# Row scatters to 64 experts: GpSimd waits for every two of them before it sends the next two

## The chip, the core and the metric

The kernel runs on one core of a Trainium2 chip. The metric is the device time of one execution in microseconds (us). Before the change three runs took 3416.25, 3429.02 and 3433.31 us, with a median of 3429.02.

## What is computed

The program is a chain of eleven layers over x, 4096 tokens of 128 numbers. The change touches two of them, the first and the second, which are mixtures of 64 experts with a shared expert. The reference of such a layer, cut to what matters here:

```python
logits = x @ wg.T                            # 4096 tokens, 64 experts
gates = softmax(logits)
w_topk, idx_topk = top_k(gates, 8)           # eight experts for each token
w_topk = w_topk / w_topk.sum(-1)
rank  = position of the token in the list of its expert
valid = rank < 160                           # capacity of an expert
buf   = zeros(64, 160, 128).at[expert, rank].set(x[token])
h     = einsum("ech,efh->ecf", buf, expert_w1); x1, x2 = split(h)
out   = einsum("ecf,ehf->ech", x1 * silu(x2), expert_w2)
combined = zeros(4096, 128).at[token].add(w * out[expert, rank])
y = shared_expert(x) + combined
```

The program computes x = x + 0.5 * moe(layernorm(x)), then a block attention with 8 heads over blocks of 64 tokens, then the same kind of mixture again, and after that eight layers of other kinds.

## The kernel before

The tokens stand in SBUF as 32 tiles of 128 rows. Routing goes over them in 8 groups of 4 tiles. For each group VectorE computes statistics, normalized rows, gates, the eight largest, and for each row eight slot numbers (`idx`, written at L1932). A slot is a place in a table `rows` of 10240 slots (64 experts of 160) in HBM. GpSimd then writes the rows to their slots: `pool_scatter` issues, for each of the 4 tiles and each of the 8 choices, one indirect DMA of 128 rows (L1814), so 32 scatters for a group. Rows whose slot number is out of bounds are dropped. Below, such an indirect DMA is called a scatter.

`pool_send` (L1818) calls it. The first three groups (`SURE` is 3) are always sent, with two semaphores `early` in turn. Each later group is sent only if some expert is not full yet (L1831), with the semaphore `sent`, and GpSimd waits for its 32 scatters at its end (L1833). In the trace five groups are sent in the first mixture (160 scatters) and four in the second (128). The group buffers `row` and `idx` are eight deep, as many as there are groups, so no group waits for a buffer to come free.

The first mixture's routing is a stage of its own (`routing_alone`, names l0f1r). Beside it VectorE runs the steps of a state kernel for a later layer, and SP clears HBM tables. The second mixture's routing runs beside the block attention (`block_attention`, names l0a). There GpSimd's stream also holds the additions of the attention's output bias to x (`pool_residual`, L2101), 16 of them, in program order with the sends: two of them follow the first send, one follows the second. Each stage ends only when all engines are through, GpSimd with its last scatters too. Then the stage of the experts (names l0f1e, l0f2e) loads the rows back from HBM, computes, and adds the results to a table with scatters of its own (L2986, 80 rows each).

In two later layers (names l3f1a, l3f2a) another class does routing to 8 experts, with 8 scatters for a group. The change doesn't touch it.

Of the kernel before, what the change touches and what calls it, by code (L numbers as in the profile page):

```python
# [802 lines left out]
class RoutingApart:  # L803
# [6 lines left out]
    DEPTH, LATE = 4, 4  # L810
    PER = 16 * TPG * K

# [51 lines left out]
    def pool_send(self, g, n):  # L864
# [10 lines left out]
        if n:  # L875
            g.wait_ge(self.sent[1 - n % 2], self.PER * ((n + 1) // 2))
            g.sem_inc(self.rows_free, 1)
# [876 lines left out]
class Routing:  # L1754
# [6 lines left out]
    DEPTH = 8  # L1761
    NONE = 65536.0
    SURE = -(-SLOTS // (K * GT))
    PER = 16 * TPG * K

    def __init__(self, ph, c, m, front, logits, hidden, out, kept=GROUPS):
# [40 lines left out]
        g.sem_inc(self.rows_free, self.DEPTH)  # L1807
        self.last_slot = g.to_reg(SLOTS - 1)

    def pool_scatter(self, g, n, sent):  # L1810
        u = n % self.DEPTH
        for t in range(TPG):
            for j in range(self.K):
                g.indirect_dma_start(out=self.m.rows, out_offset=bass.IndirectOffsetOnAxis(  # L1814
                    ap=self.idx[u][:, t, j:j + 1], axis=0), in_=self.row[u][:, t, :], in_offset=None,
                    bounds_check=self.last_slot, oob_is_err=False).then_inc(sent, 16)

    def pool_send(self, g, n):  # L1818
        g.wait_ge(self.rows_ready, TPG * (n + 1))
        g.wait_ge(self.idx_ready, n + 1)  # L1820
        if n == 0:
            g.wait_ge(self.m.rows_cleared, self.m.ROWS_CLEARED)
        if n < self.SURE:
            self.pool_scatter(g, n, self.early[n % 2])
            if n:
                g.wait_ge(self.early[1 - n % 2], self.PER * ((n + 1) // 2))
                g.sem_inc(self.rows_free, 1)
            return
        g.wait_ge(self.full_ready, n - self.SURE + 1)
        least = g.value_load(self.full[n % self.DEPTH][0:1, 0:1], min_val=0, max_val=TOKENS)  # L1830
        with g.If(least < self.CAP):  # L1831
            self.pool_scatter(g, n, self.sent)
            g.wait_ge(self.sent, self.PER * (n - self.SURE + 1))  # L1833
        if n == self.SURE:
            g.wait_ge(self.early[1 - self.SURE % 2], self.PER * ((self.SURE + 1) // 2))
            g.sem_inc(self.rows_free, 1)
        g.sem_inc(self.rows_free, 1)
# [79 lines left out]
    def dve_slots(self, v, n):  # L1917
# [4 lines left out]
                               op0=ALU.is_lt, op1=ALU.mult)  # L1922
        if n >= self.SURE:
            V.tensor_reduce(self.least[:, :], self.rank[:, 0:E], AX_X, ALU.min).then_inc(self.least_ready, 1)
# [2311 lines left out]
```

## Time and profile before

| | before |
|---|---|
| median of 3 runs | 3429.02 us |
| the profiled execution, first to last instruction (its span) | 3818.2 us |
| TensorE busy in it | 2748.8 us |
| VectorE busy | 2054.0 us |
| ScalarE busy | 1399.8 us |
| GpSimd busy | 1883.3 us |
| mean granted TensorE clock | 0.819 |

The trace is of one execution, and it is the only one whose inside is seen. The page gives its span and no total for what lies around it. The span is 389 us longer than the median of the runs. Busy time counts the running of instructions, not their waits; for a scatter GpSimd is busy while it makes the transfer's descriptors, and not while the data moves. A stretch of the trace is shown with the busy time and the number of instructions of each engine in it, in the order TensorE, its weight loads, VectorE, ScalarE, GpSimd. After these come the granted TensorE clock (1.00 is 2.4 GHz, 0.50 is 1.2 GHz), the busy share of the 16 DMA engines, and GB/s.

### The profile page before, as it was taken

The numbers are of one execution on the slowest core, as the hardware profiler recorded it, in microseconds if no ns is written. First come the engines' busy times: TensorE is split into PE (matmuls) and PEld (weight loads), VectorE is DVE, ScalarE is ACT, GpSimd is POOL, SyncE is SP. The second block draws the span as 40 slices with busy tenths as digits, with TensorE's granted clock in tenths as the row PEclk, the third lists the DMA queues.
The fourth block names the chain that finished last, engine by engine and source line by source line (L and its number), as shares of the span: only waits on it lengthen the run. The fifth ranks groups of instructions, "written<-read, shape, count | busy, mean of one in ns | idle before, by whom it ended". The sixth has DMA issues, their size and how long they took to land. (4 is left out here: it accounts for less than half of the span.)

```text
span 3818.2 us, 69208 instructions
## 1 busy us (share of the span) xinstructions
PE 2748.8 (72%) x24495; PEld 1757.8 (46%) x24514; DVE 2054.0 (54%) x6095; ACT 1399.8 (37%) x2956; POOL 1883.3 (49%) x2224
## 2 busy tenths in 40 slices
PE   1226994543889565889988999764688876998763
PEld 1114883332578533555546554453233333555453
DVE  4356334432623354468854776312699998776313
ACT  1111221210222131436643655323667662654323
POOL 5651774345057531249973123354588885133354
PEclk7667997665799877979978998687799997998586
DMA  9101994110069674111000101122212120110123
GB/s 364 34 1 38 222 223 101 50 57 10 26 168 221 167 248 117 69 19 18 18 6 12 21 21 27 36 70 74 84 56 89 45 89 13 19 27 23 35 73 92
DMA packets 222726, 294.16 MB, mean 77 GB/s; under 512 B 36704, under 2 KB 179583, under 8 KB 216288
## 3 DMA queue, kind: packets, MB, share of 16 engines
q1 hardware_dynamic: 168544, 245.65, 20.6%
q0 software_dynamic: 47616, 39.44, 5.5%
q10 hardware_dynamic: 6272, 5.24, 0.6%
q8 instruction: 173, 2.83, 0.3%
q14 instruction: 121, 0.99, 0.1%
HBM read 181.88 MB, written 107.12 MB: 76 GB/s over the span
## 5 line engine op out<-in xcount | busy, mean ns | idle before, releaser
L3694 POOL TENSOR_TENSOR l3am_db<-l3am_du,l3am_bs 128x512 f32<-128x512 f32 x256 | 318.4, 1274 | 44.9 <-DVE l3am_hh L3915 44.1
L4034 PE MATMUL l3am_y<-l3am_hc,ident 128*128 128x512 f32 x512 | 280.7, 631 | 82.1 <-DVE l3am_hc L3923 81.0
L3915 DVE TENSOR_TENSOR_SCAN l3am_hh<-l3am_dA,l3am_db 128x512 f32<-128x512 f32 x256 | 299.7, 1206 | 21.4 <-ACT l3am_dA L3824 12.0
L1161 POOL TENSOR_TENSOR l2a_pT<-l2a_pT,kept 128x512 int32<-128x512 int32 x224 | 278.7, 1278 | 63.1 <-ACT l2a_pT L1367 63.1
L2986 POOL DMA_INDIRECT l0f_table<-l0f2e_y,l0f2e_idx x128 | 178.9, 1398 | 179.3 <-DVE l0f2e_idx L2958 131.8
L2986 POOL DMA_INDIRECT l0f_table<-l0f1e_y,l0f1e_idx x128 | 178.9, 1398 | 144.2 <-DVE l0f1e_idx L2958 96.4
L1248 DVE CUSTOM_DVE_ANT_0 l2a_junk<-l2a_s,addend 128x256 f32<-128x256 f32 x512 | 188.3, 421 | 65.4 <-PE l2a_s L1484 60.3
L1814 POOL DMA_INDIRECT l0f_rows<-l0f1r_row,l0f1r_idx x160 | 160.0, 1000 | 104.1 <-issue 69.5
L1241 DVE TENSOR_REDUCE l3f2a_mx<-l3f2a_s 128x2 f32<-128x512 f32 x256 | 166.2, 685 | 55.2 <-PE l3f2a_s L1484 53.2
L1367 ACT ACTIVATE l3f2a_pT<-l3f2a_e 128x512 f32<-128x512 f32 x256 | 141.8, 596 | 144.1 <-PE l3f2a_e L1501 113.4
L1367 ACT ACTIVATE l3f1a_pT<-l3f1a_e 128x512 f32<-128x512 f32 x256 | 141.7, 596 | 142.7 <-PE l3f1a_e L1501 100.2
L1241 DVE TENSOR_REDUCE l3f1a_mx<-l3f1a_s 128x2 f32<-128x512 f32 x256 | 165.8, 685 | 52.4 <-PE l3f1a_s L1484 50.3
L4034 PEld LDWEIGHTS l3am_y<-l3am_hc,ident 128*128 128x128 f32 x512 | 94.7, 198 | 206.7 <-DVE l3am_hc L3923 147.6
L3824 ACT ACTIVATE l3am_dA<-l3am_dl,l3am_al 128x512 f32<-128x512 f32 x256 | 167.3, 682 | 58.4 <-POOL l3am_dl L3683 29.8
L1501 PE MATMUL l2a_e<-l2a_qk 32*128 32x256 f32 x1024 | 178.0, 429 | 11.3 <-DVE l2a_pT L1169 11.3
L1501 PE MATMUL l3f2a_e<-l3f2a_qk 32*128 32x256 f32 x1024 | 181.6, 450 | 2.7 <-issue 2.0
L1484 PE MATMUL l3f2a_s<-l3f2a_qk 32*128 32x256 f32 x1024 | 180.3, 452 | 3.4 <-issue 2.4
L1484 PE MATMUL l3f1a_s<-l3f1a_qk 32*128 32x256 f32 x1024 | 177.7, 442 | 6.4 <-issue 3.1
L1501 PE MATMUL l3f1a_e<-l3f1a_qk 32*128 32x256 f32 x1024 | 180.2, 443 | 1.0 <-ACT l3f1a_pT L1367 0.6
L1484 PE MATMUL l2a_s<-l2a_qk 32*128 32x256 f32 x1024 | 168.5, 440 | 4.2 <-DMA l2a_qk<-l2a_none 4.2
L3923 DVE TENSOR_TENSOR l3am_hc<-l3am_hh,l3am_c 128x512 f32<-128x512 f32 x256 | 161.0, 669 | 2.5 <-remote 1.6
L1814 POOL DMA_INDIRECT l0f_rows<-l0a_row,l0a_idx x128 | 125.0, 976 | 69.5 <-issue 60.8
(821 smaller groups left out, 6995.2 us busy)
## 6 DMA issues: line engine op xcount, KB each, us to landing
l3am_bs<-l3a_b SPq DMA_DIRECT2D x32, 1024.0 KB, 6.3
l0f1m_w<-in_L_ffn_expert_w SPq DMA_DIRECT2D x64, 384.0 KB
l0f2m_w<-in_L_ffn_expert_w SPq DMA_DIRECT2D x64, 384.0 KB
l0f_rows<-blank SPq DMA_DIRECT2D x8, 1930.0 KB, 15.3
l0f1m_w<-in_L_ffn_expert_w SPq DMA_DIRECT2D x64, 192.0 KB
l0f2m_w<-in_L_ffn_expert_w SPq DMA_DIRECT2D x64, 192.0 KB
l1a_top<-l1a_kernel SPq DMA_DIRECT2D x12, 1024.0 KB, 11.9
l3f_rows<-blank SPq DMA_DIRECT2D x8, 1440.0 KB, 12.5
```

The costliest lines, as they stand in the source:

```text
L1161: self.nc.gpsimd.tensor_tensor(t, t, self.kept[:, f // 8 % 2, :].unsqueeze(1).to_broadcast([P, 2, 2 * P]), ALU.mult).then_inc(self.cut_g, 1)
L1241: self.nc.vector.tensor_reduce(self.mx[n % 3][:, t, col:col + 2], self.sb_[f % 3][:, :].rearrange("p (h s) -> p h s", h=2), AX_X, ALU.max) ...
L1248: m = self.nc.vector.tensor_tensor_reduce(out=self.junk[:, 2 * (f % 2) + q, :], in0=self.sb_[f % 3][:, 2 * P * q:2 * P * q + 2 * P], in1=s ...
L1367: self.nc.scalar.activation(self.pT[f % self.NP][:, :], self.eb[f % 3][:, :], ACT.Exp).then_inc(self.p_ready, 1)
L1484: m = self.nc.tensor.matmul(self.sb_[f % 3][:, 2 * P * q:2 * P * q + 2 * P], self.qk[n % 4][rows, s, 0, t * P:(t + 1) * P], self.qk[n % 4] ...
L1501: m = self.nc.tensor.matmul(self.eb[f % 3][:, 2 * P * q:2 * P * q + 2 * P], self.qk[b % 4][rows, s, 1, kh * P:(kh + 1) * P], self.qk[b % 4 ...
L1814: g.indirect_dma_start(out=self.m.rows, out_offset=bass.IndirectOffsetOnAxis(ap=self.idx[u][:, t, j:j + 1], axis=0), in_=self.row[u][:, t, ...
L2986: g.indirect_dma_start(out=tables[p], out_offset=bass.IndirectOffsetOnAxis(ap=idx[u % RING][:, a:a + 1], axis=0), in_=y[u % RING][:, a, :] ...
L3694: G.tensor_tensor(db[j][n % 2][:, :], du[j][k % 2][:, :], bs[s // QUARTER][:, s % QUARTER, :], ALU.mult).then_inc(db_ready[j], 1)
L3824: A.activation(dA[j][n % 2][:, :], dl[j][k % 2][:, :], ACT.Exp, scale=al[:, j, s:s + 1]).then_inc(dA_ready, 1)
L3915: V.tensor_tensor_scan(hh[j][n % 2][:, :], dA[j][n % 2][:, :], db[j][n % 2][:, :], 0.0, ALU.mult, ALU.add).then_inc(h_ready, 1)
L4034: T.matmul(yb[j][:, :], c.ident[:, :], hc[j][n % 2][:, :], start=(s == 0), stop=(s == N - 1)).then_inc(summed, 1)
```

## The change

`pool_scatter` gets a number `landed`, the count that the semaphore had before the group. It adds 16 for each scatter, and after every second scatter GpSimd waits until the semaphore has reached it. So two scatters are sent, both have to arrive, and only then come the next two. For the groups behind the first three the wait at the end of the group was there before and is now the last of the sixteen. All lines below move down by one to three.

```diff
@@ Routing
+    AT_ONCE = 2
@@ pool_scatter
-    def pool_scatter(self, g, n, sent):
+    def pool_scatter(self, g, n, sent, landed):
         u = n % self.DEPTH
         for t in range(TPG):
             for j in range(self.K):
                 g.indirect_dma_start(out=self.m.rows, out_offset=bass.IndirectOffsetOnAxis(
                     ap=self.idx[u][:, t, j:j + 1], axis=0), in_=self.row[u][:, t, :], in_offset=None,
                     bounds_check=self.last_slot, oob_is_err=False).then_inc(sent, 16)
+                landed += 16
+                if j % self.AT_ONCE == self.AT_ONCE - 1:
+                    g.wait_ge(sent, landed)
@@ pool_send
-            self.pool_scatter(g, n, self.early[n % 2])
+            self.pool_scatter(g, n, self.early[n % 2], self.PER * (n // 2))
...
-            self.pool_scatter(g, n, self.sent)
-            g.wait_ge(self.sent, self.PER * (n - self.SURE + 1))
+            self.pool_scatter(g, n, self.sent, self.PER * (n - self.SURE))
```

GpSimd's stream in the routing stage before, from the first scatter of group 0 to the first of group 2. `early0` and `early1` are the two semaphores of the groups in turn, and `x31` stands for 31 like instructions in a row.

```order
L1814 DMA l0f_rows<-l0f1r_row,l0f1r_idx 10240x193 [waits l0f1_rows_cleared,l0f1r_idx_ready,l0f1r_rows_ready]
L1814 DMA l0f_rows<-l0f1r_row,l0f1r_idx 10240x193 x31
L1814 DMA l0f_rows<-l0f1r_row,l0f1r_idx 10240x193 [waits l0f1r_idx_ready,l0f1r_rows_ready]
L1814 DMA l0f_rows<-l0f1r_row,l0f1r_idx 10240x193 x31
L1814 DMA l0f_rows<-l0f1r_row,l0f1r_idx 10240x193 [waits l0f1r_early0,l0f1r_idx_ready,l0f1r_rows_ready]
```

The same stream now, its first six scatters:

```order
L1815 DMA l0f_rows<-l0f1r_row,l0f1r_idx 10240x193 [waits l0f1_rows_cleared,l0f1r_idx_ready,l0f1r_rows_ready]
L1815 DMA l0f_rows<-l0f1r_row,l0f1r_idx 10240x193
L1815 DMA l0f_rows<-l0f1r_row,l0f1r_idx 10240x193 [waits l0f1r_early0]
L1815 DMA l0f_rows<-l0f1r_row,l0f1r_idx 10240x193
L1815 DMA l0f_rows<-l0f1r_row,l0f1r_idx 10240x193 [waits l0f1r_early0]
L1815 DMA l0f_rows<-l0f1r_row,l0f1r_idx 10240x193
```

No scatter has moved to another place. Every second one now carries a wait for the two ahead of it.

In the attention's stage GpSimd's stream before, from the last bias additions ahead of the first send to the third send:

```order
L2101 TENSOR_TENSOR x_state<-x_state,l0a_bo 128x256 [waits l0f1e_o_done] x12
L1814 DMA l0f_rows<-l0a_row,l0a_idx 10240x193 [waits l0f2_rows_cleared,l0a_idx_ready,l0a_rows_ready]
L1814 DMA l0f_rows<-l0a_row,l0a_idx 10240x193 x31
L2101 TENSOR_TENSOR x_state<-x_state,l0a_bo 128x256 [waits l0f1e_o_done] x2
L1814 DMA l0f_rows<-l0a_row,l0a_idx 10240x193 [waits l0a_idx_ready,l0a_rows_ready]
L1814 DMA l0f_rows<-l0a_row,l0a_idx 10240x193 x31
L2101 TENSOR_TENSOR x_state<-x_state,l0a_bo 128x256 [waits l0a_early0,l0f1e_o_done]
L1814 DMA l0f_rows<-l0a_row,l0a_idx 10240x193 [waits l0a_idx_ready,l0a_rows_ready]
```

And now, the last bias addition and the two sends around it, at their ends:

```order
L1815 DMA l0f_rows<-l0a_row,l0a_idx 10240x193 [waits l0a_early1]
L1815 DMA l0f_rows<-l0a_row,l0a_idx 10240x193
L2104 TENSOR_TENSOR x_state<-x_state,l0a_bo 128x256 [waits l0a_early1,l0a_early0,l0f1e_o_done]
L1815 DMA l0f_rows<-l0a_row,l0a_idx 10240x193 [waits l0a_idx_ready,l0a_rows_ready]
L1815 DMA l0f_rows<-l0a_row,l0a_idx 10240x193
L1815 DMA l0f_rows<-l0a_row,l0a_idx 10240x193 [waits l0a_early0]
```

The bias additions stand at the same places among the sends, and the last one now also waits for the second group's own last two scatters (`early1`).

## Rows read from the trace of the kernel before

**Rows 1.** The cores view: the span of the one core.

```profile
core 0: 3818.2 us, clock 0.819
```

**Rows 2.** Page, part 5: line engine op, tiles, count | busy us, mean ns | idle before.

```profile
L1814 POOL DMA_INDIRECT l0f_rows<-l0f1r_row,l0f1r_idx x160 | 160.0, 1000 | 104.1 <-issue 69.5
L1814 POOL DMA_INDIRECT l0f_rows<-l0a_row,l0a_idx x128 | 125.0, 976 | 69.5 <-issue 60.8
```

**Rows 3.** Stretches: window, length, busy (x count) by engine, PEclk, DMA share, GB/s.

```profile
30.00:274.00 244.00, 59.71 (x231) 36.08 (x230) 96.14 (x364) 28.24 (x38) 159.38 (x160) 0.64 0.31 113
278.00:354.00 76.00, 37.40 (x148) 23.00 (x148) 63.86 (x152) 11.55 (x16) 0.00 (x0) 0.72 0.00 0
370.00:590.00 220.00, 201.44 (x1600) 188.80 (x1598) 67.44 (x186) 48.39 (x123) 171.60 (x124) 1.00 0.89 217
...
1640.00:1990.00 350.00, 332.70 (x3936) 186.09 (x3936) 251.10 (x1200) 191.78 (x379) 286.89 (x251) 0.88 0.09 15
...
2705.00:3180.00 475.00, 383.85 (x947) 161.33 (x964) 443.94 (x521) 315.39 (x500) 385.34 (x330) 0.95 0.18 72
```

**Rows 4.** Stretches, same columns: the block attention, by scatter group.

```profile
717.00:758.00 41.00, 11.94 (x96) 6.40 (x80) 3.40 (x18) 0.88 (x3) 31.01 (x32) 0.50 0.22 75
758.00:780.00 22.00, 15.71 (x407) 10.61 (x407) 14.38 (x61) 6.96 (x20) 1.50 (x3) 0.73 0.13 32
...
906.00:947.00 41.00, 11.68 (x106) 6.35 (x105) 1.02 (x3) 1.72 (x5) 31.07 (x32) 0.51 0.03 2
947.00:1064.00 117.00, 94.01 (x849) 61.79 (x848) 67.17 (x260) 28.19 (x56) 0.00 (x0) 0.78 0.06 22
```

**Rows 5.** Timeline of TensorE, routing beside gqa: start, us, what [idle before <-releaser].

```profile
2255.82 1.09 PE L1451 MATMUL l3f1a_misc<-ident,l3f1a_oU 128*128 128x128 f32 x4 [3.15 <-issue]
```

**Rows 6.** Timeline of GpSimd: group 3 of l0f1r, then the last scatter there.

```profile
232.22 0.98 POOL L1814 DMA_INDIRECT l0f_rows<-l0f1r_row,l0f1r_idx  x1 [21.62 <-issue]
233.50 0.98 POOL L1814 DMA_INDIRECT l0f_rows<-l0f1r_row,l0f1r_idx  x1 [0.30 <-issue]
...
273.69 0.98 POOL L1814 DMA_INDIRECT l0f_rows<-l0f1r_row,l0f1r_idx  x1 [0.30 <-issue]
```

**Rows 7.** Stretches around that last scatter: is the DMA share above zero?

```profile
275.00:275.20 0.20, 0.00 (x0) 0.00 (x0) 0.00 (x0) 0.00 (x0) 0.00 (x0) 0.50 0.00 0
275.20:275.40 0.20, 0.00 (x0) 0.00 (x0) 0.00 (x0) 0.00 (x0) 0.00 (x0) 0.50 0.12 2
275.40:275.60 0.20, 0.00 (x0) 0.00 (x0) 0.00 (x0) 0.00 (x0) 0.00 (x0) 0.50 0.02 0
275.60:276.00 0.40, 0.00 (x0) 0.00 (x0) 0.00 (x0) 0.00 (x0) 0.00 (x0) 0.50 0.00 0
```

**Rows 8.** Timeline of GpSimd: first scatter of l0f1r; two of the experts' scatters.

```profile
32.63 1.17 POOL L1814 DMA_INDIRECT l0f_rows<-l0f1r_row,l0f1r_idx  x1 [22.12 <-DVE l0f1r_idx L1932]
...
371.01 1.45 POOL L2986 DMA_INDIRECT l0f_table<-l0f1e_y,l0f1e_idx  x1 [0.30 <-issue]
...
376.78 1.40 POOL L2986 DMA_INDIRECT l0f_table<-l0f1e_y,l0f1e_idx  x1 [0.92 <-DMA l0f_table<-l0f1e_y,l0f1e_idx]
```

**Rows 9.** DMA view, 32.6 to 38.7: queue, packets, MB, share (q0 is GpSimd's).

```profile
q1 hardware_dynamic: 1028, 2.36, 100.3%
q0 software_dynamic: 49, 0.10, 4.6%
```

**Rows 10.** Stretches of the start, columns as in rows 3.

```profile
75.00:90.00 15.00, 1.12 (x4) 0.72 (x4) 2.65 (x11) 1.88 (x2) 11.40 (x12) 0.50 1.01 360
90.00:100.00 10.00, 0.00 (x0) 0.00 (x0) 0.89 (x8) 0.00 (x0) 7.56 (x9) 0.50 0.41 146
```

**Rows 11.** Stretches inside the first scatter group of l0a, columns as before.

```profile
722.00:732.00 10.00, 4.03 (x25) 2.03 (x25) 0.00 (x0) 0.00 (x0) 7.76 (x8) 0.50 0.23 79
732.00:742.00 10.00, 2.45 (x11) 1.38 (x10) 0.00 (x0) 0.66 (x2) 7.67 (x8) 0.50 0.23 79
742.00:752.00 10.00, 1.48 (x5) 1.05 (x6) 0.00 (x0) 0.00 (x0) 7.56 (x9) 0.50 0.23 79
```

## What was predicted

> **What bounds the kernel now.** I began with the cores view and the medians. The one execution whose inside is seen spans 3818.2 us [rows 1], the timed runs take 3429.02, so 389 us of the trace can't be in a timed run. Before any stage is read as a bound, the place of those 389 us has to be found.
>
> The table by line shows what the change touches: 160 scatters of 1000 ns in the first mixture and 128 of 976 ns in the second, back to back but for "issue" idle [rows 2]. Then I read the stretches. The experts' stage and the two long later ones are full: TensorE busy 201.44 of 220 us, 332.70 of 350, 383.85 of 475 with VectorE at 443.94 [rows 3]. Little can be missing there in a timed run. It is otherwise where scatters go out. In the first 244 us of routing VectorE is busy 96.14 us, right after the last scatter 63.86 of 76 [rows 3]. In the attention, a 41-us stretch with a group of scatters holds 96 TensorE instructions, the next 22 us without them 407 [rows 4]. Inside such a stretch TensorE issues 25, then 11, then 5 instructions in 10 us [rows 11]; even the bursts of 8 scatters in the later mixtures have a matmul that waits 3.15 us on "issue" [rows 5]. So in the profiled execution everything but GpSimd nearly stands still while scatters are on their way.
>
> I try the guess that this stall is the excess. Without it the first routing loses 354 − 240 = 114 us (240 is worked out below), the attention its four stretches, 4 × 41 = 164, and the later mixtures perhaps 16 bursts × 3.15 = 50. Together that is 328 of the 389. Nothing else in the rows is large and loose enough. I take it that timed runs have little of the stall, and lay out both stages anew without it.
>
> First routing, timed: VectorE has 96.14 + 63.86 = 160 us of work from 30 on; at the share it reaches undisturbed, 63.86/76 = 0.84, it is through after 190 us, at 220 to 230. GpSimd has 160 scatters, one each 233.50 − 232.22 = 1.28 us (0.98 busy, 0.30 issue) [rows 6], from 32.63 [rows 8]: 32.6 + 160 × 1.285 = 238, plus landing, 240. GpSimd is the bound by 10 to 20 us. In the attention the others end at 1064 − 164 = 900 (1064 ends the last stretch of [rows 4]), GpSimd at 717 + 128 × 1.285 + 2 = 884, 16 us ahead of them. So the first stage has no cover for a slower GpSimd, and the second 16 us.
>
> **What the change does.** It removes nothing and moves no instruction. It adds a wait for the arrival of every pair: 80 in the first mixture, 64 in the second. A pair takes 2 × 1.285 = 2.57 us now. With the wait it takes one issue step, 1.285, then the landing of the second scatter, then a restart.
>
> Landing, quiet: the last scatter starts at 273.69 [rows 6] and DMA is last above zero in the slice that ends at 275.60 [rows 7]: 1.9 us. Restart: 0.2 us, an estimate, less than the 0.30 us of an ordinary issue step [rows 6]. Pair: 1.29 + 1.9 + 0.2 = 3.4 us, 0.83 more than now. Bounds: 3.1, if the semaphore comes a little before the last packet's end and restart is free; 3.7, if restart is a full 0.3 and landing 2.1.
>
> Landing beside full queues: until about 90 us the clears take all DMA (share 1.01 from 75 to 90, 0.41 from 90 to 100) [rows 10]. The first scatter starts at 32.63 [rows 8], and in the window up to 38.7 GpSimd's queue shows just 49 packets [rows 9], where each scatter has 48: it took 6.0 us. The experts' stage gives the same from another side: there two scatters are followed by a wait now, and 371.01 to 376.78 is 5.77 us at a DMA share of 0.89 [rows 8, 3]. So a loaded pair takes 1.29 + 6.0 = 7.3 us.
>
> A page of the Trainium skill has a milder rule. "DMA: Bandwidth & Descriptors", section "Latency and other measured facts", puts the memory's access at 0.2 us on average and 2 us at high load, inside a fixed cost of some 2.0 us. By an estimate from that page a loaded landing would be 4 us, a loaded pair 5.3, and the first stage would lose 85 us and not 96. The trace disagrees: 6.0 us.
>
> First mixture: from 32.6 to 90 there are 57.4/7.3 = 8 loaded pairs; 72 × 3.4 = 245 us follow; GpSimd ends at 90 + 245 + 1 = 336, against 240: **+96**. Bounds: no load and 3.1, 32.6 + 248 = 281, +41; load and 3.7, 90 + 266 = 356, +116. Nothing hides it, as VectorE is through by 230 and the stage ends with GpSimd's scatters. No group waits for a buffer (eight deep), so VectorE isn't held up either.
>
> Second mixture: DMA share beside the scatters is 0.23 and later 0.03 [rows 11, 4], so all pairs are quiet: 717 + 64 × 3.4 + 2 = 937 against 900: **+37**. The 16 us of cover are used in it. Bounds: 3.1 gives 917, +17; 3.7 gives 956, +56. Behind the waits stand the bias additions in GpSimd's stream. The one that follows the second group comes at 717 + 109 = 826 in place of 799. Even if every other engine waited for it and ended 27 us later, at 927, GpSimd would still be last. The groups behind the first three had a wait at their end before, which is merged into the new one: nothing.
>
> The terms are steps between two layouts without the stall, so they stand against the median, and not against 3818.2. The sum is 3429 + 96 + 37 = 3562. In the profiled execution, where the stall is, the same change may come out otherwise (below).
>
> **Rivals.** (A) Faster. The stall is in the timed runs too, and a wait relieves it. For it: in the experts' stage GpSimd is busy 171.60 of 220 us with scatters of its own and waits after each two, yet TensorE is busy 201.44 us there [rows 3]. So what stalls the others could be a pile of unlanded scatters, and TensorE's decay, 25, 11, 5, looks like a growing pile [rows 11]. Price: the first stage ends at 340 and not 354, −14; the attention ends with GpSimd at 937 and not at 1064, −127; 3429 − 141 = 3288. It decides from the point where a timed run loses more to stalls than the 133 us that GpSimd's chain grows. Against it: the 389 us. With the full stall in timed runs they would have to come out of stretches that are full. A smaller share of the stall gives something between, so I would not be surprised by 3300 to 3420.
>
> A rule of the Trainium skill speaks against any stall by memory: "SBUF — State Buffer", section "Who interferes with whom", says only VectorE and GpSimd share a pair of ports and that TensorE and ScalarE wait on nobody, nor does DMA contend with an engine. By it rival A has no mechanism in a timed run, and no price. The trace shows TensorE all but stopped beside scatters, so in the profiled execution the rule doesn't hold as it stands.
>
> (B) No change. The trace is to be taken as it is, stages bound by stalled engines, and the stall goes with the number of scatters and not with their time. GpSimd then ends at 336 to 345 in a stage that ends at 354, and its last group, started at 906, at 906 + 16 × 3.4 + 2 = 963 in a stage that ends at 1064: all hidden, 3429. Against it again the 389 us.
>
> (C) Slower in another way. The stall is in timed runs and lasts as long as scatters go out. The first stage then ends 78 us after the last of them (354 − 275.6), at 336 + 78 = 414, +60; in the attention each stretch grows from 41 to 54.5, +54: 3543. For it is the decay in [rows 11], against it the experts' stage.
>
> (D) Slower by less. The mechanism is mine, but what else runs in a timed first stage ends near 300 and not 230, or the wait isn't for the whole landing: +20 to +80, about 3480.
>
> **Chances.** My forecast 0.58, A 0.16, B 0.11, C 0.08, D 0.07. A measurement of this kernel tells no change from about 0.5%, 17 us. Faster is A, 0.16; same is B with nothing else, 0.11; slower is the rest, 0.73. The likeliest case's own range is the sum of the bounds, +58 to +172, so 3487 to 3601. The range to hold 8 in 10 goes down to B and a little more and up past C and my upper bound: 3415 to 3610; it leaves out most of A and some 0.03 above.
>
> **What would show it.** In the changed profile: every second scatter released by its own semaphore, with pairs 3.4 us apart after 90 us and about 7 before; the last scatter of the first mixture at about 335; in the attention 54 to 55 us for a group. If TensorE and VectorE stay stalled beside the scatters, the profiled span grows too, by 50 to 120 us; if they run on at the rate of 758 to 780, the wait relieves a pile, and the span falls, perhaps by more than 100 us, while the timed runs still get slower. That split, profile shorter and timed longer, would be the strongest sign that the stall belongs to the profiled execution. The forecast is wrong if pairs come at under 2.9 us, if VectorE and not GpSimd ends the first stage in a run without the stall, or if timed runs get faster, which says that they had the stall.

## The result: 213 us slower, in a condition that the profile of before doesn't show

The changed kernel takes 3643.73 us (3638.84 to 3649.49, 4 runs), the kernel before, in the same comparison, 3431.16 us. The ratio is 1.0635, with a 95% interval of 1.0593 to 1.0677 (the two medians alone give 1.062). The direction was as forecast. The size wasn't: 3562 was said, with 3610 as the upper end.

Two things have to be kept apart from here on. The profile of before, with its span of 3818.2 us [rows 1], is not of the condition in which either time was taken. The kernel before was profiled a second time (`e1_again` below) and its span came out at 3436.1, beside a median of 3420.99. One of that run's ten executions took 4459.47 us at a granted clock of 0.547, where the others had 0.85 to 0.86, and it is left out of the ratio. On three other chips the kernel before had medians of 3819.76, 3801.96 and 3812.68 us. So the kernel has two times. This text calls them the free condition (3430) and the stalled one (3800 to 3820). The result is of the free one. The rows ahead of the prediction are of the stalled one. The chips of the result and of the profile of before aren't on record, and each of the four chips of the experiments was used in one session only, so it isn't shown whether the chip itself or something that changes with time sets the condition.

### The profile page after: what moved, and what is told of

It reads as the page before. It is cut to its first block and busy times, and to the rows that moved or that the text cites. A ratio compares the mean times of both kernels' runs of the same rounds, so it can differ in the third digit from the quotient of the medians.

```text
span 3638.3 us, 69228 instructions
## 1 busy us (share of the span) xinstructions
PE 2656.1 (73%) x24514; PEld 1706.3 (47%) x24514; DVE 2056.4 (57%) x6095; ACT 1401.1 (39%) x2956; POOL 1884.8 (52%) x2224
## 5 line engine op out<-in xcount | busy, mean ns | idle before, releaser
L3697 POOL TENSOR_TENSOR l3am_db<-l3am_du,l3am_bs 128x512 f32<-128x512 f32 x256 | 318.2, 1274 | 46.3 <-DVE l3am_hh L3918 45.5
L1815 POOL DMA_INDIRECT l0f_rows<-l0f1r_row,l0f1r_idx x160 | 162.5, 1016 | 199.3 <-DMA l0f_rows<-l0f1r_row,l0f1r_idx 146.9
L1815 POOL DMA_INDIRECT l0f_rows<-l0a_row,l0a_idx x128 | 124.8, 975 | 128.2 <-DMA l0f_rows<-l0a_row,l0a_idx 105.5
L1501 PE MATMUL l3f1a_e<-l3f1a_qk 32*128 32x256 f32 x1024 | 172.0, 434 | 0.6 <-ACT l3f1a_pT L1367 0.6
L1501 PE MATMUL l3f2a_e<-l3f2a_qk 32*128 32x256 f32 x1024 | 172.0, 434 | 0.6 <-ACT l3f2a_pT L1367 0.6
L1484 PE MATMUL l3f2a_s<-l3f2a_qk 32*128 32x256 f32 x1024 | 171.5, 437 | 0.4 <-DVE l3f2a_mx L1241 0.4
## 6 DMA issues: line engine op xcount, KB each, us to landing
l0f1m_w<-in_L_ffn_expert_w SPq DMA_DIRECT2D x64, 384.0 KB, 3.2
l0f2m_w<-in_L_ffn_expert_w SPq DMA_DIRECT2D x64, 384.0 KB
```

The source lines that it names most:

```text
L1484: m = self.nc.tensor.matmul(self.sb_[f % 3][:, 2 * P * q:2 * P * q + 2 * P], self.qk[n % 4][rows, s, 0, t * P:(t + 1) * P], self.qk[n % 4] ...
L1501: m = self.nc.tensor.matmul(self.eb[f % 3][:, 2 * P * q:2 * P * q + 2 * P], self.qk[b % 4][rows, s, 1, kh * P:(kh + 1) * P], self.qk[b % 4 ...
L3697: G.tensor_tensor(db[j][n % 2][:, :], du[j][k % 2][:, :], bs[s // QUARTER][:, s % QUARTER, :], ALU.mult).then_inc(db_ready[j], 1)
```

## The profile after

Page, the cores view and part 5 of the changed kernel (columns as in [rows 1, 2]):

```profile
core 0: 3638.3 us, clock 0.833
```

```profile
L1815 POOL DMA_INDIRECT l0f_rows<-l0f1r_row,l0f1r_idx x160 | 162.5, 1016 | 199.3 <-DMA l0f_rows<-l0f1r_row,l0f1r_idx 146.9
L1815 POOL DMA_INDIRECT l0f_rows<-l0a_row,l0a_idx x128 | 124.8, 975 | 128.2 <-DMA l0f_rows<-l0a_row,l0a_idx 105.5
```

The scatters are as long as in [rows 2]. What is new is their idle time, which now ends with the arrival of a scatter: 146.9 and 105.5 us.

Stretches of the changed kernel (columns as in [rows 3]), the first routing up to VectorE's end and behind it, then the attention beside the scatters, and its end:

```profile
30.00:228.00 198.00, 94.69 (x381) 57.63 (x380) 161.06 (x519) 40.78 (x55) 86.16 (x82) 0.75 0.36 138
228.00:372.00 144.00, 0.00 (x0) 0.00 (x0) 0.00 (x0) 0.00 (x0) 75.64 (x78) 0.50 0.02 4
740.00:806.00 66.00, 50.59 (x1576) 35.74 (x1578) 53.23 (x235) 24.11 (x71) 31.23 (x33) 0.90 0.24 71
...
955.00:998.00 43.00, 0.00 (x0) 0.00 (x0) 0.00 (x0) 0.00 (x0) 22.92 (x24) 0.52 0.02 1
```

VectorE is through at 228. For 144 us more only GpSimd works, at a TensorE clock of 0.50 and a DMA share of 0.02. The experts' stage starts at 377.3. Beside the attention the other engines run freely, with 1576 TensorE instructions in 66 us against 96 in 41 [rows 4]. They are through at 954.1, and GpSimd is not: its last scatter starts at 998.50, and the experts follow at 1005.1.

GpSimd's timeline in the changed kernel, at the start beside the clears, where scatters carry rows, and late, where all their rows are dropped (start, us, what, [idle before <-releaser]):

```profile
32.98 1.17 POOL L1815 DMA_INDIRECT l0f_rows<-l0f1r_row,l0f1r_idx  x1 [22.12 <-DVE l0f1r_idx L1935]
34.45 0.99 POOL L1815 DMA_INDIRECT l0f_rows<-l0f1r_row,l0f1r_idx  x1 [0.30 <-issue]
40.94 0.98 POOL L1815 DMA_INDIRECT l0f_rows<-l0f1r_row,l0f1r_idx  x1 [5.50 <-DMA l0f_rows<-l0f1r_row,l0f1r_idx]
...
141.79 0.98 POOL L1815 DMA_INDIRECT l0f_rows<-l0f1r_row,l0f1r_idx  x1 [1.73 <-DMA l0f_rows<-l0f1r_row,l0f1r_idx]
143.08 1.04 POOL L1815 DMA_INDIRECT l0f_rows<-l0f1r_row,l0f1r_idx  x1 [0.30 <-issue]
145.80 1.22 POOL L1815 DMA_INDIRECT l0f_rows<-l0f1r_row,l0f1r_idx  x1 [1.69 <-DMA l0f_rows<-l0f1r_row,l0f1r_idx]
...
370.43 0.98 POOL L1815 DMA_INDIRECT l0f_rows<-l0f1r_row,l0f1r_idx  x1 [1.39 <-DMA l0f_rows<-l0f1r_row,l0f1r_idx]
371.71 0.98 POOL L1815 DMA_INDIRECT l0f_rows<-l0f1r_row,l0f1r_idx  x1 [0.30 <-issue]
```

The first pair takes 40.94 − 32.98 = 7.96 us, and the first five, which stand beside the clears, 46.3 us together, 9.3 each. Later a pair takes 145.80 − 141.79 = 4.01 where it carries rows, and 3.64 (the median of the last two groups) where nothing is written. The prediction had 7.3, 3.4 and 3.4.

DMA view of the changed kernel, the scatters of four stretches: count, median us from issue to landing. The first routing at 100 to 190 (with rows) and at 250 to 370 (empty), then the attention at 740 to 805 (with rows) and at 955 to 998 (empty):

```profile
l0f_rows<-l0f1r_row,l0f1r_idx POOLq DMA_INDIRECT x44, 2.5
l0f_rows<-l0f1r_row,l0f1r_idx POOLq DMA_INDIRECT x64, 2.1
...
l0f_rows<-l0a_row,l0a_idx POOLq DMA_INDIRECT x31, 2.6
l0f_rows<-l0a_row,l0a_idx POOLq DMA_INDIRECT x24, 2.1
```

## The experiments

All ratios are to the kernel before, run beside them on the same chip. The first four ran in the free condition, on one chip, all others in the stalled one, on three chips. The condition can't be chosen. Where a stage's length is given, it runs from its first instruction to the first of the next stage.

### The kernel before again

No edit.

> This is the kernel before, unchanged, so that its profiled execution can be seen a second time. Theory 1 (the stall beside scatters belongs to profiled executions that hold many scatters in flight): the median is 3430 again, and the profiled span is again near 3818, with 41-us stretches in the attention in which TensorE issues about 100 instructions. Theory 2 (the 3818.2 us execution was a single one out of the ordinary): the profiled span is about 3428 this time, the first routing ends at about 240, and the attention with its routing takes about 272 us in place of 437.

Measured: 3420.99 us, ratio 0.999 (0.9958 to 1.0022), span 3436.1. Theory 2 holds as far as this chip goes. The cores view and stretches of this execution, the first routing up to VectorE's end and on to the last scatter, then three scatter groups of the attention (the first, second and fourth) and what is behind them:

```profile
core 0: 3436.1 us, clock 0.854
```

```profile
30.00:228.00 198.00, 95.20 (x380) 57.82 (x379) 160.77 (x518) 40.77 (x55) 148.58 (x145) 0.75 0.38 140
228.00:247.00 19.00, 0.00 (x0) 0.00 (x0) 0.12 (x1) 0.00 (x0) 14.43 (x16) 0.50 0.05 11
614.00:654.00 40.00, 32.33 (x936) 22.94 (x927) 32.11 (x143) 14.48 (x42) 30.46 (x32) 0.87 0.32 99
656.00:697.00 41.00, 27.77 (x804) 19.64 (x792) 30.78 (x140) 12.91 (x39) 31.38 (x34) 0.80 0.33 96
739.00:779.00 40.00, 39.61 (x183) 24.62 (x182) 20.56 (x57) 11.14 (x18) 30.27 (x32) 1.00 0.03 2
779.00:797.00 18.00, 16.29 (x91) 11.26 (x89) 5.79 (x9) 2.98 (x5) 0.97 (x1) 1.00 0.01 1
```

This is the layout that the prediction worked out of the stalled trace. VectorE ends at 228 (said: 220 to 230). GpSimd's last scatter starts at 246.86, and the experts' stage at 252.5 (said: 240). The attention's stage lasts from 523.5 to 797.8, which is 274.2 us; 626.6 to 900 had been worked out, 273.4. There GpSimd has cover: from its last scatter to the next stage it needs 998.50 to 1005.1, 6.6 us, in the changed kernel, so here it could have ended the stage at 779.0 + 6.6 = 785.6, and 797.8 − 785.6 = 12.2 us are to spare (said: 16).

### The waits in one mixture, and in the other

```diff
-                if j % self.AT_ONCE == self.AT_ONCE - 1:
+                if (self.K * t + j + 1) % self.AT_ONCE == 0 and (self.AT_ONCE < 32 or n >= self.SURE):
...
+        at.r.AT_ONCE = 32                     # e2_alone: the Routing beside the attention
...
+        r.AT_ONCE = 32                        # e3_beside: the Routing of routing_alone
```

(32 leaves only the wait at the end of each later group, which was there before.)

> The waits after each two scatters stand in the first mixture's routing alone (80 of them); beside the attention there are none. Theory 1 (each stage ends with GpSimd, and each loses its own waits): in the changed kernel the first routing ended at 377 where 240 was worked out for before, so this kernel loses 125 to 140 of the 212 us and takes about 3563. Theory 2 (the first stage was ended by VectorE at about 230 to 300 in timed runs, and most of the loss is in the attention): 3490 or less.

> The waits after each two scatters stand beside the attention alone (64 of them); the first routing has none. Theory 1: the rest of the 212 us, about 79, so 3510; the two single kernels' losses add up to the whole one. Theory 2 (the other stage holds most of it): 3580 or more. If the two losses sum to much less than 212, then something that both stages share, such as when a later stage's loads are ready, takes part.

Measured: 3555.07 us, ratio 1.0371 (1.0295 to 1.0447), and 3496.86, ratio 1.022 (1.0141 to 1.0299). That is +128 and +70, together 198 beside 213 for both at once, which the intervals allow. In the traces the experts' stage starts at 380.2 with the waits and 252.0 without, and the attention's stage takes 359.6 and 279.1. Theory 1 of each holds: each stage pays for itself.

### A wait after eight

```diff
-    AT_ONCE = 2
+    AT_ONCE = 8
```

> A wait after every eight scatters, so 20 waits in the first mixture and 16 in the second, in place of 80 and 64. Theory 1 (the cost is a landing for each wait, nothing else): a quarter of the 212 us and a little more where queues are loaded, less the cover of about 16 us that the attention has: +35 to +55, so about 3475. Theory 2 (the cost is that of a chain of one pair at a time, in which the landing grows because GpSimd's descriptors go out in small lots): less than in proportion, under +25.

Measured: 3481.23, ratio 1.0167 (1.0099 to 1.0234), +54. Theory 1 holds at its upper end. The first routing grows by 43.8 us for 20 waits. Three of them stand beside the clears, where the steps of 7.2, 13.0 and 7.2 us in place of 1.28 make 24 us of it. The attention grows by 290.4 − 274.2 = 16.2. There the last scatter starts 28.3 us later in the stage than in the kernel before, and the stage ends 16.2 later: 12.1 us were covered, as read from the second profile of before.

### A wait after each

```diff
-    AT_ONCE = 2
+    AT_ONCE = 1
```

> A wait after each scatter, so 160 and 128 waits in place of 80 and 64. Theory 1 (a wait costs the whole time from the start of the scatter ahead to its landing and the restart, less the 1.28 us issue step: in the changed kernel's trace 2.75 us for scatters with rows, 2.37 for empty ones): scatters stand 2.75 and 2.37 us apart, two of them take 1.4 or 1.1 us more than a pair does now, the first routing grows by about 100 and the attention by about 85 more: 3640 + 185 = 3825. Theory 2 (a lone scatter lands sooner than the second of a pair, since it shares the queues with nothing): steps of about 2.2 us, and 3740 to 3760.

Measured, in the stalled condition: 3966.72, ratio 1.0405 (1.0351 to 1.0458). GpSimd's timeline there, on empty scatters:

```profile
419.60 0.98 POOL L1815 DMA_INDIRECT l0f_rows<-l0f1r_row,l0f1r_idx  x1 [1.37 <-DMA l0f_rows<-l0f1r_row,l0f1r_idx]
421.96 0.98 POOL L1815 DMA_INDIRECT l0f_rows<-l0f1r_row,l0f1r_idx  x1 [1.39 <-DMA l0f_rows<-l0f1r_row,l0f1r_idx]
```

They stand 2.36 us apart, as theory 1 has it (2.37), so a scatter lands no sooner alone than as the second of a pair. The experts' stage starts at 486.5, 102 later than in the changed kernel in the same condition (`c1_changed` below; said: 100), and the attention's takes 447.4 us, 82 more (said: 85). The time in the free condition that was forecast (3825) can't be set against this run, where the later routings stall.

### The waits beside the clears

```diff
-                if j % self.AT_ONCE == self.AT_ONCE - 1:
+                if (self.K * t + j + 1) % self.AT_ONCE == 0 and n >= self.FREE:
...
+        r.FREE = 1                            # in routing_alone; 0 beside the attention
```

> As the changed kernel, but the 16 waits of the first group of the first mixture, whose scatters go out while the tables are cleared, are left out. Theory 1 (waits beside the clears cost far more than others: there 5 pairs took 46 us): the first routing gets shorter by 38 to 50 us, a third of the loss of 125 from a fifth of the waits, and the time is about 3598. Theory 2 (the clears matter little, each of the 80 waits costs 1.5 us): 25 us, 3618. A wait of over 8 us is expected at the first pair of the second group, where the backlog has to land.

Measured: 3732.88, ratio 0.9789 (0.9738 to 0.984), in the stalled condition. Only the stage can be compared: the experts start at 344.9, against 382.1 in `e8_dropped`, which has all the waits in this routing and ran beside it. That is 37.2 us for 16 waits, just under the 38 to 50 of theory 1 and well above the 25 of theory 2. GpSimd's timeline at the second group's first waits:

```profile
75.56 0.98 POOL L1816 DMA_INDIRECT l0f_rows<-l0f1r_row,l0f1r_idx  x1 [0.30 <-issue]
86.31 0.98 POOL L1816 DMA_INDIRECT l0f_rows<-l0f1r_row,l0f1r_idx  x1 [9.78 <-DMA l0f_rows<-l0f1r_row,l0f1r_idx]
87.60 0.98 POOL L1816 DMA_INDIRECT l0f_rows<-l0f1r_row,l0f1r_idx  x1 [0.30 <-issue]
92.97 0.98 POOL L1816 DMA_INDIRECT l0f_rows<-l0f1r_row,l0f1r_idx  x1 [4.39 <-DMA l0f_rows<-l0f1r_row,l0f1r_idx]
```

A part is paid back at once, as the backlog has to land first: 9.78 and 4.39 us.

### The rows dropped

```diff
-        self.last_slot = g.to_reg(SLOTS - 1)
+        self.last_slot = g.to_reg(self.LAST)
...
+        at.r.LAST = 0                         # beside the attention; SLOTS - 1 in the first mixture
```

> As the changed kernel, but in the second mixture every scatter has its upper bound on slots set to 0, so that all rows but one are dropped; the number of scatters, waits and slots computed is unchanged, and the experts of that mixture then work on blank rows. Theory 1 (what a scatter carries sets 0.4 us of its landing): all pairs in the attention stand 3.65 us apart, also in the first groups, where they are 4.0 to 4.6 now, and that stage ends 20 to 25 us sooner, 333 us after its start in place of 357. Theory 2 (the attention's own loads in the queues make the landing longer): pairs in the first groups stay at 4.0 or more, and the stage stays within 8 us of 357.

Measured: 3757.35 us, ratio 0.9854 (0.9789 to 0.992), again in the stalled condition. The medians of a pair in the attention's four groups are 3.67, 3.64, 3.64 and 3.65 us, and with rows (`c1_changed`, the changed kernel in the stalled condition) 4.56, 4.00, 3.73 and 3.64. The stage takes 348.0 in place of 365.1 us. Theory 1 holds in the medians. Some single pairs of 4.2 to 7.4 us stay in the first two groups, so the stage gains 17 us and not 20 to 25. In the second group the rows account for 4.00 − 3.64 = 0.36 us of a pair, in the first, with 0.89, for more. That the pairs that stay long do so because of neighbours in the queues is likely and wasn't tested.

### A few waits under cover

```diff
+        r.AT_ONCE = 32
+        at.r.AT_ONCE = 16
```

> No added waits in the first mixture, and beside the attention one after every 16 scatters, 8 in all, each worth 1.4 us by the pairs' rows. In the kernel before, seen a second time, the last scatter beside the attention starts 12 us before the time from which it would end the stage. Theory 1 (the first 12 us are covered by the other engines' work): the last scatter starts 11 to 12 us later, the stage stays at 274 us, the time within 3 us of before. Theory 2 (each wait is paid in full): the stage grows by 10 to 12 us.

> Waits after each 16 scatters beside the attention alone, again; the first run was beside a before of 3820, where the stall hides what it was to tell. Where before takes 3430: theory 1 (12 us of cover, 8 waits of 1.4 us) the last scatter starts 11 to 12 us later in the stage, which stays at 274 us, and the time is within 5 us of before. Theory 2 (each wait paid in full): stage and time grow by 10 to 12 us. Where before takes 3800: the same time as before, again, since lots of 16 stall as fully as lots of 32.

Measured twice, both in the stalled condition: 3819.1, ratio 0.9997 (0.9972 to 1.0023), and 3810.94, ratio 0.999 (0.9974 to 1.0006). For the cover this says nothing, since there the others end the stage; `e5_tile` is what shows it. It says something else: lots of 16 stall the others as lots of 32 do, with the attention's stage at 434 and 436 us. GpSimd's timeline of `e9_cover` at the first wait there, behind 16 scatters in a row:

```profile
740.85 0.97 POOL L1815 DMA_INDIRECT l0f_rows<-l0a_row,l0a_idx  x1 [0.31 <-issue]
743.62 0.97 POOL L1815 DMA_INDIRECT l0f_rows<-l0a_row,l0a_idx  x1 [1.79 <-DMA l0f_rows<-l0a_row,l0a_idx]
```

The sixteenth scatter had landed 2.77 us after its start, restart included, as soon as the second of a pair does. So nothing piles up beside the attention in the stalled condition either.

### The changed kernel in the stalled condition

No edit, then the lots of eight and of four.

> The changed kernel again. The kernel before took 3427 us beside the first experiments and 3820 beside the last ones, where it shows the stall of the profile of before; so this is read against the before that runs beside it. Theory 1 (the stall is a property of the chip or its condition, it is in timed runs there, and a wait after two scatters relieves it wholly in the two mixtures): where before takes 3820, the changed kernel takes about 3780, so it is faster by 1%, as the routing ends at 377 and the attention's stage takes 357 on either; where before takes 3430, it takes 3640 again. Theory 2 (the waits don't touch the stall): 3820 + 212 = 4030 where before takes 3820.

> The kernel with a wait after each eight scatters in the two mixtures, again. Theory 1: where before takes 3820, a burst of 8 costs the others about 5 us, as in the later routings (41 us for 8 bursts), so 20 bursts put the first routing's VectorE at 228 + 100 = 328 and 16 bursts the attention at 273 + 80 = 353: 3820 - 30 - 80 = 3710. Where before takes 3430: 3481 as before. Theory 2 (eight stall as fully as 32): no gain against the before beside it, 3820 or more.

```diff
-    AT_ONCE = 2
+    AT_ONCE = 4
```

> A wait after each four scatters. By the pairs' rows a wait costs 1.45 us with rows and 1.1 empty, and about 4 beside the clears: 40 waits in the first routing cost 60 to 75 us, 32 in the attention 42 less 12 of cover. Where before takes 3430: 3525. Where before takes 3820, theory 1 (a pile of four stalls little): the first routing ends at 325 and the attention takes 305, so 3820 - 35 - 130 = 3655, better than the waits after two and after eight. Theory 2 (four stall as eight do, each burst 2.5 us): both stages end with the others, and 3700 to 3720.

| lot | time, ratio (interval) | experts start | attention's stage |
|---|---|---|---|
| none (`c2_later`, same chip) | before: 3801.96 | 358.7 | 437.6 |
| 8 | 3732.68, 0.9815 (0.9766 to 0.9864) | 296.7 | 414.7 |
| 4 | 3700.69, 0.9722 (0.967 to 0.9773) | 328.6 | 358.6 |
| 2 | 3760.34, 0.988 (0.983 to 0.9931) | 384.0 | 365.1 |

In this condition the change makes the kernel faster, by 1.2%. That is rival A of the prediction in kind and not in size or cause: a wait relieves the stall in timed runs, but they gain 42 us and not 141. The first stage gets 25 us longer, where −14 was said, the attention's 72 shorter, where −127 was said, and no pile is relieved (`e9_cover` above). Stretches in the first group beside the attention, of the kernels with lots of 8, 4 and 2 (columns as in [rows 3]; the first group of the profile of before had 96 TensorE instructions in 41 us [rows 4]):

```profile
651.00:700.00 49.00, 26.98 (x338) 15.02 (x332) 11.51 (x55) 5.12 (x15) 32.05 (x33) 0.51 0.22 72
```

```profile
690.00:740.00 50.00, 38.28 (x591) 23.04 (x591) 20.78 (x92) 8.91 (x26) 29.09 (x31) 0.60 0.23 71
```

```profile
750.00:811.00 61.00, 51.11 (x1155) 33.13 (x1157) 41.49 (x182) 17.97 (x52) 26.22 (x27) 0.72 0.22 65
```

In 10 us TensorE issues 69, 118 and 189 instructions, and 23 with lots of 32. The first routing is different: with lots of eight VectorE already ends at 229.6 us, as in the free condition. A burst of 8 was forecast to cost it 5 us each, with an end at 328, and that was wrong. It was not tested why. `c1_changed` came out 20 us below what theory 1 said (3780), `c3_tile` 23 above (3710). With four, theory 1 was off by 46 us (3655 said) since the attention takes 358.6 us and not 305.

### The later routings alone

```diff
                     bounds_check=self.last_slot, oob_is_err=False).then_inc(self.sent[n % 2], 16)
+                i = self.K * t + j + 1
+                if i % 2 == 0:
+                    g.wait_ge(self.sent[n % 2], self.PER * (n // 2) + 16 * i)
```

> The kernel before with waits after each two scatters only in the two later routings to 8 experts, whose bursts of 8 have none; GpSimd has slack there. Theory 1 (a pile of more than two unlanded scatters stalls the others): where before takes 3820, those two stages take 377 us in place of 418 each, about 80 us in all, so 3740; where before takes 3430 there is no stall to relieve and GpSimd's slack hides the waits: within 5 us. Theory 2 (the stall there is of something else): no gain where before takes 3820.

> The waits in the two later routings alone, again. Where before takes 3800: 3725 again, the two stages 360 each. Where before takes 3430: by theory 1 no stall is there to relieve, and GpSimd's slack hides the waits, so within 10 us of before; by theory 2 bursts of 8 cost something there too, and it gets faster by 20 us or more, since the later routings took 377 us there and 360 with the waits.

Measured: 3724.68, ratio 0.9784 (0.973 to 0.9839), and 3730.23, ratio 0.9803 (0.9759 to 0.9846), both stalled. The first of the two stages takes 384.9 and 384.4 us, against 431.1 in `c1_changed`, and its other engines are through after 359.3 and 360.2 us, against 416.8. Both kernels came out 77 to 82 us faster, as theory 1 said. What these waits do in the free condition has not been measured. The stage up to where the other engines are through, stalled without waits, stalled with them, and free without them:

```profile
2026.00:2443.00 417.00, 375.40 (x4112) 213.13 (x4112) 264.73 (x753) 195.34 (x433) 114.03 (x276) 0.80 0.11 27
```

```profile
2073.00:2433.00 360.00, 329.77 (x4112) 194.69 (x4112) 262.80 (x756) 193.63 (x433) 111.35 (x274) 0.91 0.13 31
```

```profile
1809.00:2183.00 374.00, 347.66 (x4112) 201.77 (x4112) 262.66 (x750) 196.06 (x433) 113.93 (x276) 0.85 0.12 30
```

(The first row is of `c1_changed`, the second of `c2_later`, the third of `e1_again`.) The instructions are the same; TensorE loses its stops and gets a granted clock of 0.91 in place of 0.80. With the waits the stalled condition is even quicker here than the free one without them, 360 against 374 us, so bursts of eight may cost something in the free condition too.

### A pause in place of a wait

```diff
-    AT_ONCE = 2
+    AT_ONCE = 32
...
+                if self.PAUSE and n < self.SURE and i % 2 == 0:
...
+                    self.nc.gpsimd.memset(self.pause[:, :], 0.0).then_inc(self.paused, 1)
```

> The kernel before with no added wait on a scatter. Beside the attention, in its first three groups, a memset of 128x1024 on GpSimd (0.96 us by rows of the trace, some 1.26 with its issue step) follows each two scatters, so they go out at the pace of the changed kernel (3.8 us for a pair) without awaiting an arrival; the fourth group has none and is the comparison. Where before takes 3800 or more: theory 1 (scatters one right after another stall TensorE, whatever has landed): TensorE issues 150 instructions or more per 10 us in the first groups, about 50 in the fourth, and the stage takes about 360 us in place of 436. Theory 2 (it is unlanded scatters that stall, and only a wait for the arrival drains them): about 50 in all four groups, and a stage of 450 or more. Where before takes 3430 there is no stall, and the stage grows from 274 by 48 x 1.26 less 12 of cover, to about 322.

Measured, stalled: 3738.46, ratio 0.9802 (0.9766 to 0.9839). Stretches of its four groups beside the attention, three with the pause and the last without:

```profile
721.00:774.00 53.00, 42.18 (x763) 26.24 (x763) 30.27 (x109) 11.07 (x33) 45.51 (x47) 0.56 0.24 74
777.00:829.00 52.00, 41.57 (x738) 27.49 (x736) 31.55 (x121) 9.97 (x30) 44.79 (x47) 0.53 0.23 70
832.00:884.00 52.00, 33.16 (x582) 23.07 (x572) 33.46 (x140) 9.35 (x29) 44.80 (x47) 0.53 0.23 77
887.00:926.00 39.00, 21.09 (x66) 10.96 (x66) 13.38 (x54) 7.85 (x10) 29.86 (x31) 0.76 0.03 2
```

144, 142 and 112 instructions in 10 us with the pause, 17 without. The fourth group can't be set beside the first three as it stands, since the attention's work is another there (183 instructions in 40 us in the free condition, against 936 in the first group). The kernel before can: 96 in 41 us in its first group [rows 4]. The stage takes 358.8 us and not 436 (said: about 360). Theory 1 holds: the pace of the scatters stalls TensorE, and a gap of 0.84 us for each pair (3.4 in place of 2.56 us) takes away 79 us of stall, of some 41 for each of the three groups. No arrival of a scatter has to be awaited.

The lots of eight and four fit the same reading. By the mean length of a pair in the first group beside the attention TensorE issues 23 instructions in 10 us at 2.57 us, 69 at 2.87 (lots of eight), 118 at 3.35 (lots of four), 144 at 3.40 (the pause) and 189 at 4.67 (pairs awaited). It also explains a stage that rival A was argued from: in the first experts' stage the scatters go out 1.70 us apart (1.40 busy and 0.30 issue), and it takes 242.8 us in the profile of before and 244.5 in the second one, so it isn't stalled. At steps of 1.28 us and landings of 2.4 to 2.7 no more than two or three scatters are unlanded in the attention's stage, and `e9_cover` shows no backlog, so the "pile" of rival A and of several expectations isn't there.

### What the runs point to in the stalled condition

Lots of 8 in the first mixture, of 4 beside the attention, and of 2 in the later routings.

> What the runs point to for the condition with the stall: a wait after each 8 scatters in the first routing (its stage ended at 297, after four at 329, after two at 384), after each 4 beside the attention (358 us), and after each 2 in the two later routings (359 and 361 in place of 417). Theory 1 (the three act apart and add): where before takes 3800, 3701 - 32 - 77 = 3592. Theory 2 (what is won in the later layers or the first is lost elsewhere, as the clock is shared out over time): over 3640. Where before takes 3430: the first routing +44, the attention +25 to +35, the later ones 0 or a few less, so 3500, slower than before.

Measured: 3603.28 us, ratio 0.9457 (0.942 to 0.9493), beside a before of 3812.68. In the stalled condition that is the best of the kernels, 5.4% faster, and 11 us from the sum of its parts: theory 1. In the free condition it was not run. By `e5_tile` its first routing alone would cost 44 us there, so no kernel here is shown to beat the one before in both conditions. The waits in the later routings alone (`c2_later`) might, and are unmeasured in the free one.

## Why the prediction was right in direction and wrong in size

**The stall.** The prediction read the 389 us between span and median as stall that timed runs don't have, and gave each stage its place in it: 114, 164 and 50 us. The second profile of the kernel before gives 357.0 − 252.5 = 105 us for the first routing, 438 − 274 = 164 for the attention, and for each of the two later routings 40 (429 against 389), with 22 in each of the experts' stages behind them. So the two stages that the change touches were right, and the later layers have 125 us of stall and not 50. It was wrong about the cause. The stall isn't one of profiling. It is in every timed run on three of four chips, and absent from profiles on the fourth. The sign that the prediction called the strongest for a stall of the profiled execution, a shorter profile (3638 after 3818) with longer timed runs, came out all the same, since the profile of before was of one condition and that of after of the other.

That the direction was right rests on this in part by luck. The layout without the stall holds for the free condition, in which the comparison ran. In the stalled one the same change is 1.2% faster (`c1_changed`), and the prediction's argument gave no reason why timed runs couldn't be in it.

**The bounds of the two stages.** They were right. GpSimd ends the first (said: by 10 to 20 us; its last scatter starts at 247, VectorE is through at 228), and the attention has a cover of 12 us (said: 16). The terms add up. The bias additions behind the second group cost nothing, as the others end at 954.1, 44 us ahead of the last scatter.

**The step that failed: "Pair: 1.29 + 1.9 + 0.2 = 3.4 us".** The 1.9 us were read from the last scatter of the first mixture [rows 6, 7], which comes when the experts are full: all its rows are dropped, and its packets carry next to nothing (2 GB/s in [rows 7]). And it ends with the last packet, where GpSimd waits for the semaphore. The DMA view of the changed kernel has a median landing of 2.1 us for empty scatters and 2.5 to 2.6 for those with rows. Measured from the start of the second scatter to the next pair, an empty one takes 2.36 us and one with rows 2.7 (145.80 − 143.08), so the restart is 0.2 to 0.3 us and its estimate of 0.2 was near. The landing was the term that was too small. By pairs that makes 3.64 and 4.0, with more in the attention's first groups: the means of its groups are 4.25, 4.29, 3.87 and 3.66 us, and 4.07 over all, the steps from group to group included. The stated bounds, 3.1 and 3.7, hold an empty pair and none with rows.

**The two terms.** For the first mixture the term was +96, and it is 377.3 − 252.5 = +125. The last scatter comes at 371.7 and lets go 2.4 later, 38 us after the 336 that was said; GpSimd in the kernel before ends 9 later than the 240 that was said; 96 + 38 − 9 = 125. The part beside the clears ended 11 us sooner than laid out, with two errors against each other: a pair cost 9.3 us there and not 7.3, but there were five of them and not eight. The 75 pairs behind it took 295 us, 3.93 each with the steps between groups, where 72 were laid out at 3.4, 245 us: that is the miss. For the attention the term was +37, and it is 357.2 − 274.2 = +83: 64 × (4.07 − 3.40) = 43 us by the pairs, and 5 because the experts start 6.6 us after the last scatter and not 2. Together 208 us, of the 213 measured.

**What the other readings were worth.** The 6.0 us for a landing beside full queues were near for the first pair: in the changed kernel its second scatter starts at 34.45 and the next pair at 40.94, 6.5 us with the restart. The four pairs behind it wait 7.3 to 9.3 us. The 4 us that were estimated from the Trainium skill ("DMA: Bandwidth & Descriptors", section "Latency and other measured facts") were too few. Its other rule in the prediction, that TensorE waits on nobody ("SBUF — State Buffer", section "Who interferes with whom"), spoke against rival A. In the free condition the trace shows nothing against it: 936 TensorE instructions in 40 us beside scatters. In the stalled one TensorE is held back, 96 in 41 us [rows 4], in timed runs as in profiled ones. Whether at the ports, which that rule is about, or elsewhere, no run shows; what failed is the conclusion that timed runs have no stall.

## What to carry to other kernels

Where a span and a median differ by 10%, profile the kernel again before anything is read from the trace; which stages carry the difference can be found, but not what condition the change will be timed in. Take the price of a wait from a row of the very thing that is awaited, up to where the engine goes on: an empty scatter let GpSimd go on 0.36 us sooner than one with rows, and the price of a pair, read from the last packet of an empty one, was 0.67 us short, which times 64 was 43 us. A wait behind every pair costs its landing each time on the engine that ends the stage, and where the aim is to thin out a burst, a lot of four or eight, or other work of that engine between, does it for less.

## What the runs showed of the hardware

The same kernel took 3421 to 3431 us in the free condition and 3802 to 3820 on three chips in the stalled one. The difference stands where GpSimd sends indirect DMAs one 1.28 us step after another: beside the attention's first group TensorE issues 23 instructions in 10 us, and 234 in the free condition. Scatters 1.70 us apart in the first experts' stage cost it nothing (242.8 us against 244.5). Bursts of 16 and 32 do it alike (434 to 438 us for the attention's stage, against 274), bursts of 8, 4 and 2 less and less (69, 118 and 189 instructions in 10 us), and it goes by their pace: with a 0.97 us memset between pairs TensorE issued 144. Empty scatters do it too: in the attention's fourth group TensorE is busy 11.68 of 41 us [rows 4], and 39.61 of 40 in the free condition. VectorE in the first routing bore lots of eight without loss (229.6 us against 228). Why the conditions differ, and what stops TensorE in the stalled one, stays open: no run tells it apart.
